# Dealing the last head group's maxima over 18 steps in place of 16, with the projection chain moved to match

## The chip, the cores and the metric

One core of a Trainium2 chip runs the kernel. The time is the device time of one execution in microseconds (us), from the first to the last instruction with what lies around them. The engines work side by side, each through its own list of instructions in order: TensorE (PE; its weight loads are PEld), VectorE (DVE), ScalarE (ACT), GpSimd (POOL) and SyncE (SP), which only issues transfers here. They wait for each other through semaphores, and an instruction that waits holds up all that stand behind it on its engine.

## The reference, cut to what matters

```
h = layernorm(x) * (1 + ca) + sa                      # x: 2048 tokens, 128 features
q, k, v = split(h @ W_attn + b_attn)                  # 16 heads of 8 features
att = softmax(q @ k.T / sqrt(8) + alibi_and_causal_mask)
x = x + ga * ((att @ v) @ W_proj + b_proj)
h = layernorm(x) * (1 + cb) + sb
probs = softmax(h @ router_w.T)                       # 8 experts, the best 2 are taken
y = silu(h @ w1[e]) @ w2[e] * expert_scale[e]         # 512 hidden features
x = x + gb * sum over the two experts of weight * y
```

The softmax is exact: each row's maximum is found and taken off before the exponential. The weights `ga`, `gb`, `sa` and so on come from a small conditioning product.

## The kernel before, in words

The heads are worked in four groups of four (`g` = 0 to 3). Tokens are cut into four chunks of 512 (`j`, or `c` in the later part), chunks into blocks of 128. The maxima of a row must be known before its exponentials, so attention has two passes over the scores.

**Pass 1, maxima.** A group has 72 tasks (`TASKS`, `NTASK`). A task multiplies a block row of queries by a chunk of keys on TensorE (line 724, masks at 697), into one of two slots of PSUM, and VectorE reduces it to row maxima (line 1040). When the last task of a chunk is done, VectorE makes the negated maxima (`nmax`, line 1048), GpSimd cuts them into three bf16 pieces (`cut_maxima`, lines 1445 to 1451), TensorE turns them (`turn`, line 746), ScalarE copies them to `rows` (line 1299), and SyncE sends them with four transfers into the stack of query rows `aug` (line 418). The scores of pass 2 then come with the maxima already taken off. The first step of a chunk waits for these rows (`rows_in`).

**Pass 2, steps.** A group has 36 steps (`STEPS`): chunk 0 starts at step 0, chunk 1 at 3, chunk 2 at 10, chunk 3 at 21 (`START`). A step has two halves `b`. In each half TensorE makes scores for keys by queries (line 795) into a ring of three PSUM slots, ScalarE takes exponentials (line 1326, four in a step), and TensorE multiplies the exponentials of the step before by the values (line 761). ScalarE copies a finished chunk out (`copy_values`, line 1293).

**The plan.** `plan` (line 98) says how many tasks of pass 1 are to be issued by the end of each half-step; it deals them by the share of pass 2 that has passed. Pass 1 runs `LEAD` = 41 tasks ahead, so that a group's pass 2 carries the first pass of the next. The last group (`g` = 3) has only its own 31 tasks left, numbers 41 to 71, and is done with them when the plan reaches 72, at the end of step 15. `turns` tells after which step a chunk's maxima are turned: the first step by which its tasks and four more are planned.

**What fills the second half of the last group.** From there on tables of step numbers place the next phase, for the first three chunks, into the steps on TensorE: `PROJECT` (line 648, two matmuls in each half), `TURN` (the normalized tokens, line 602), `LOGITS` (line 665) and `COUNT` (lines 674 and 677, which count tokens per expert; count 0 is for chunk 0, count 1 for chunks 1 and 2). `project` uses the PSUM banks of pass 1, so the first projection must come after the last task. VectorE has no steps there: it follows a fixed list. For each chunk it adds the projection (`residual`, line 1065), takes statistics, scales tokens after GpSimd's `deviation` (lines 1376 and 1385; then line 945), keeps the logits (1072) and ranks experts (`route`, 1082 to 1107). `place_part(0)` waits for count 0 and `place_part(1)` for count 1; they give each token its place in the tiles of its expert (1129 to 1144). Their order on VectorE is

```
residual(2)
place_part(0)
scale_tokens(2)
for k in range(1, 5):
    route(1, k)
...
place_part(1)
for j in range(DEEP - 1):
    stage(j)
```

`stage` copies an expert's first weights for a tile (line 1169), three tiles ahead at first, a fourth (`stage(3)`) only after `route(c, 5)` and the last chunk's `scale_sums`. GpSimd sends the tokens to their places with indirect transfers (`send_part`, lines 1480 and 1487): part 0 after `place_part(0)`, part 1 after `place_part(1)`; the deviation of the last chunk stands in the middle of part 1, behind twelve sends.

**The loop over 53 tiles** follows: TensorE turns a tile (870), multiplies by the first weights (`up`, 879), ScalarE takes silu (1353), TensorE multiplies by the second weights (`down`, 896), VectorE keeps the result (1177). The last chunk's projection, turn, logits and count stand among the tiles. At the end GpSimd gathers the results and VectorE joins them.

`ROUTE_EXP` places small exponentials of the routing on ScalarE at (step, exponential).

Of the kernel before, what the change touches and what calls it, by code (L numbers as in the profile page):

```python
# [44 lines left out]
NSTEP = len(STEPS)  # L45
# [7 lines left out]
NTASK = len(TASKS)  # L53
# [40 lines left out]
PASSED = [sum(PASS2[:p]) for p in range(NSTEP + 1)]  # L94
LEAD = max(TSTART[j + 1] + SETTLE + AHEAD - NTASK * PASSED[START[j]] // PASSED[NSTEP] for j in range(NC_))


def plan(first):

    if first:
        knots = [(PASSED[START[j]], TSTART[j + 1] + SETTLE0 + AHEAD0) for j in range(NC_)] + [(PASSED[NSTEP], NTASK + LEAD)]
        knots[1:1] = [(PASSED[1], TSTART[2] + SETTLE0)]
    else:
        knots = [(0, LEAD), (PASSED[NSTEP], NTASK + LEAD)]
    rows_ = []
    for p in range(NSTEP):
        row = []  # L110
        for b in range(PAIRS):
            x = PASSED[p] + PASS2[p] * (b + 1) // PAIRS
            for (x0, y0), (x1, y1) in zip(knots, knots[1:]):
                if x0 <= x <= x1:
                    want = y0 + (y1 - y0) * (x - x0) // (x1 - x0)
            row.append(want)
        rows_.append(row)
    return rows_


PLAN = {first: plan(first) for first in (True, False)}


def turns(p, first, last):

    found = []
    for u in range(2 * NC_ if not last else NC_):
        settled = TSTART[u % NC_ + 1] + NTASK * (u // NC_) + (SETTLE0 if first and u < NC_ else SETTLE)  # L130
        if first and u == 0:
            at = -1
        elif settled <= (0 if first else LEAD):
            continue
        else:
            steps = [q for q in range(NSTEP) if PLAN[first][q][-1] >= settled]
            if not steps:
                continue
            at = steps[0]
        if at == p:  # L140
            found.append(u)
    return found
# [12 lines left out]
LAST_OUT, LAST_IN, LAST_INVERT, LAST_BACK, LAST_INVERSE = [5, 11], [6, 12], [INVERT, 14], [9, 15], [10, 16]  # L155
LAST_SCALE = {13: 0, 18: 1}
DEVIATION_AT = {19: 0, 20: 1}
PROJECT = {16: 0, 18: 1, 23: 2}
TURN = {18: 0, 20: 1, 26: 2}
LOGITS = {19: 0, 21: 1, 27: 2}  # L160
ROUTE_EXP = {(20, 4): (0, 0), (23, 2): (1, 0), (25, 2): (0, 1), (28, 2): (2, 0), (30, 2): (1, 1), (34, 4): (2, 1)}
COUNT = {24: 0, 30: 1}


PARTS = [(0, TPC), (TPC, 3 * TPC), (3 * TPC, NT)]
# [50 lines left out]
def build(nc, a):  # L216
# [3 lines left out]
    with ExitStack() as ctx:  # L220
# [369 lines left out]
        def _(pe):  # L590
# [4 lines left out]
            for n, m in enumerate((0, 1, 3, 4)):  # L595
                last = mm(b1[:, 3, n:n + 1], wmod[:, m * C:(m + 1) * C], sil[:, :], start=True, stop=True)
# [87 lines left out]
            def group(g, first, last):  # L684
# [131 lines left out]
                def step(p):  # L816
                    if p == 0:
                        for u in turns(-1, first, last):
                            pass1(TSTART[u + 1] + SETTLE0)
                            turn(u)  # L820
                            pass1(TSTART[u + 1] + SETTLE0 + AHEAD0)
                    if p < NSTEP:
                        j, kbs = STEPS[p]
                        for b in range(PAIRS):
                            if p == START[j] and b == 0:
                                take(pe, rows_in[j % 2], HG * 16)
                            scores_and_maxima(p, b, min(PLAN[first][p][b], NTASK) if last else PLAN[first][p][b])
                            if p not in START:
                                value_products(p, b)
                            elif (p or g) and b == 0:  # L830
                                for half in range(PAIRS):
                                    value_products(p, half)
                                if p == 0 and not last:
                                    pe.sem_inc(aug_free, 1)
                            if last and p in PROJECT:
                                if p == min(PROJECT) and b == 0:
                                    assert at[0] == NTASK
                                    pe.wait_ge(s1_free, n_task[0] + SLOTS)
                                for half in range(2):
                                    project(PROJECT[p], 2 * b + half)  # L840
                        for u in turns(p, first, last):
                            turn(u)
                    if last:
                        if p in TURN:
                            turn_late(TURN[p])
                        if p in LOGITS:
                            logits(LOGITS[p])
                        if p in COUNT:
                            count(COUNT[p])
                    if last and p == NSTEP:  # L850
                        for b in range(PAIRS):
                            value_products(p, b)
# [70 lines left out]
        def _(dve):  # L923
# [94 lines left out]
            def group(g, first, last):  # L1018
                n_task, at = 0, 0 if first else LEAD
                for p in range(-1, NSTEP + 1):  # L1020
                    upto = PLAN[first][p][-1] if 0 <= p < NSTEP else 0
                    if last:
                        upto = min(upto, NTASK)
                    if g and p == INVERT:
# [6 lines left out]
                    while at < upto:  # L1031
                        k = at % NTASK
                        j, c, rs, b = TASKS[k]
# [574 lines left out]
```

## Time and profile before

| what | us |
|---|---|
| median of three runs | 560.79 (560.79 to 562.58) |
| the profiled execution, its time | 560.09 |
| its span, first to last instruction | 558.2 |
| busy in the span: PE, DVE, ACT, POOL | 490.7, 446.2, 396.6, 169.9 |
| last group of heads, from its first exponential | 340.58 |
| last maxima reduced on VectorE | 379.12 |
| attention ends (last copy of values begins) | 431.95 |
| last tile's products end, then gathers and joins | about 540 |

Read it by place: a busy share is a mean over phases that differ. What counts is which engine the others wait for in a stretch, and what stands behind the waiting instruction.

### The profile page before, as it was taken

To read this page: it belongs to the slowest core of one execution; us is meant where nothing else is said; L and a number is where in the kernel's file an instruction comes from. 1 tells how busy PE (TensorE), PEld (TensorE's weight loads), DVE (VectorE), ACT (ScalarE), POOL (GpSimd) and SP (SyncE) were. 2 spreads that over 40 slices of the span, in tenths; PEclk is the share of its full clock that TensorE was granted. 3 is DMA by queue.
4 is the path that set the end of the run, shared out by engine and by line. 5 is a ranking of instruction groups with operands and counts; after the bars stand their busy time and mean duration, and the time that the engine had idled before them with its cause. 6 is when DMAs were issued, how large, how long until landed. Compare 5 with 4: busy or idle time off the path is not lost.

```text
span 558.2 us, 16358 instructions
## 1 busy us (share of the span) xinstructions
PE 490.7 (88%) x6452; PEld 287.1 (51%) x6452; DVE 446.2 (80%) x775; ACT 396.6 (71%) x775; POOL 169.9 (30%) x293
## 2 busy tenths in 40 slices
PE   3756778889999999999999999999999998999960
PEld 2422233244344454444454445445434998999960
DVE  3689999989999999999999998995687646554442
ACT  3932366668989899898898897888789555555530
POOL 3410000000104112320044101066068852860864
PEclk9975799999999999999999999999899999999995
DMA  6593112000001460041320000010232222442432
GB/s 162 186 323 81 31 36 53 1 3 3 7 12 46 95 261 4 2 153 34 82 40 4 2 3 2 16 25 7 73 100 68 79 84 59 114 123 71 113 102 60
DMA packets 38267, 37.93 MB, mean 68 GB/s; under 512 B 7088, under 2 KB 33904, under 8 KB 37560
## 3 DMA queue, kind: packets, MB, share of 16 engines
q1 hardware_dynamic: 35808, 32.26, 20.3%
q0 software_dynamic: 2048, 4.20, 2.7%
q8 instruction: 53, 0.87, 0.7%
q10 hardware_dynamic: 336, 0.42, 0.2%
q14 instruction: 22, 0.18, 0.1%
HBM read 20.05 MB, written 16.61 MB: 66 GB/s over the span
## 4 chain that ended last, share of the span: by engine, by line
PE 55%; DVE 14%; ACT 5%; issue 2%; POOL 1%; DMA 1%; ACTq 0%; POOLq 0%; DVEq 0%
PE pv L761 18%; PE b L795 11%; DVE part L1040 9%; PE b L879 8%; PE b L896 8%; PE b L724 6%; ACT probs L1326 3%; PE b L697 3%; POOL raw L1508 1%; PE b L870 1%; ACT raw L1293 1%; DMA raw<-y_scratch,spots 0%; PE b L648 0%; PE b L746 0%; PE b L602 0%
## 5 line engine op out<-in xcount | busy, mean ns | idle before, releaser
L1326 ACT ACTIVATE probs<-b 128x512 f32<-128x512 f32 (+1 forms) x576 | 294.7, 571 | 65.1 <-PE b L795 29.9
L1040 DVE TENSOR_REDUCE part<-b 128x2 f32<-128x1024 f32 (+2 forms) x320 | 322.1, 1060 | 18.0 <-PE b L697 9.1
L761 PE MATMUL pv<-probs,v_cur 128*32 128x256 f32 (+1 forms) x2432 | 175.4, 370 | 0.0
L795 PE MATMUL b<-aug 55*128 55x256 bf16 (+1 forms) x1216 | 153.7, 264 | 9.3 <-ACT probs L1326 8.7
L724 PE MATMUL b<-aug 52*128 52x512 bf16 (+3 forms) x640 | 142.1, 364 | 20.5 <-DVE part L1040 18.3
L795 PEld LDWEIGHTS b<-aug 55*128 55x128 bf16 x1216 | 56.9, 94 | 119.6 <-ACT probs L1326 105.0
L761 PEld LDWEIGHTS pv<-probs,v_cur 128*32 128x32 f32 x2432 | 50.0, 108 | 49.7 <-ACT probs L1326 24.2
L724 PEld LDWEIGHTS b<-aug 52*128 52x128 bf16 x640 | 42.9, 94 | 39.8 <-DVE part L1040 29.8
L879 PE MATMUL b<-hTt,inverse 128*128 128x128 f32 x424 | 56.3, 276 | 0.8 <-ACT hTt L1347 0.8
L896 PE MATMUL b<-w2T_sb,hst 128*128 x424 | 56.2, 276 | 0.8 <-ACT hst L1353 0.8
L896 PEld LDWEIGHTS b<-w2T_sb,hst 128*128 128x128 f32 x424 | 51.6, 192 | 1.2 <-issue 1.2
L879 PEld LDWEIGHTS b<-hTt,inverse 128*128 128x128 f32 x424 | 51.5, 192 | 1.1 <-issue 1.0
L1353 ACT ACTIVATE hst<-b 128x512 f32<-128x512 f32 x53 | 31.6, 597 | 21.9 <-PE b L879 21.9
L1169 DVE COPY inverse<-aug 128x512 f32 x53 | 25.1, 474 | 24.4 <-issue 19.0
L1445 POOL CAST nmp<-nmax 128x16 bf16<-128x16 f32 x16 | 3.4, 211 | 124.6 <-POOLq L192 124.6
L1347 ACT ACTIVATE hTt<-b,modc 128x128 f32<-128x128 f32 x53 | 24.1, 456 | 22.7 <-PE b L870 22.7
L697 PE MATMUL b<-maskQ,identh 64*128 64x64 bf16 (+1 forms) x512 | 40.1, 210 | 0.0
L1177 DVE TENSOR_TENSOR aug<-b,gate 128x128 f32<-128x128 f32 x53 | 15.4, 290 | 25.4 <-PE b L896 22.8
L1487 POOL DMA_INDIRECT slot_scratch<-slots,spots x32 | 32.6, 1017 | 9.0 <-POOL pause L1480 9.0
L1480 POOL MEMSET pause<- 128x512 f32 (+1 forms) x56 | 25.4, 453 | 31.6 <-DMA y_scratch<-aug 29.6
L1508 POOL DMA_INDIRECT raw<-y_scratch,spots x32 | 31.2, 975 | 11.7 <-POOL pause L1480 6.8
L697 PEld LDWEIGHTS b<-maskQ,identh 64*128 64x128 bf16 x512 | 30.4, 99 | 6.6 <-issue 1.8
(151 smaller groups left out, 368.6 us busy)
## 6 DMA issues: line engine op xcount, KB each, us to landing
xt<-slot_scratch SPq DMA_DIRECT2D x53, 64.0 KB, 2.0
y_scratch<-aug SPq DMA_DIRECT2D x53, 64.0 KB, 1.6
slot_scratch<-slots SPq DMA_DIRECT2D x3, 1024.0 KB, 8.4
aug<-q_scratch SPq DMA_DIRECT2D x6, 384.0 KB
aug<-k_scratch SPq DMA_DIRECT2D x6, 384.0 KB
w2T_sb<-in_w2T SPq DMA_DIRECT2D x1, 2048.0 KB, 8.1
aug<-in_w1T SPq DMA_DIRECT2D x8, 256.0 KB
q_scratch<-pieces SPq DMA_DIRECT2D x4, 384.0 KB, 2.8
```

The lines of the kernel that those rows point to most:

```text
L697: return mm(bank[:, at_ + c0:at_ + c1], identh[k, h, :], table[k, h, c0:c1], start=False, stop=True, skip_group_check=True)
L724: ins = mm(bank[:, at_:at_ + w], q_aug[buf][n, b, t:t + P], k_aug[buf][n, b, c * CW:c * CW + w], start=True, stop=True)
L761: return mm(pv[32 * hh:32 * hh + 32, c0:c1], v_cur[:, kb, hh, :], probs[:, step_ % 2, hh, at_:at_ + c1 - c0], start=(kb == 0 and c0 == 0), ...
L795: ins = mm(bank[:, at_:at_ + w], k_aug[g % 2][n, pair, kb * P:kb * P + P], q_aug[g % 2][n, pair, j * CW + c0:j * CW + c1], start=True, sto ...
L879: last = mm(b1[:, j % 2, f * P:(f + 1) * P], w1s[:, k, f * P:(f + 1) * P], hTt[:, j % 2, :], start=True, stop=True)
L896: last = mm(b1[:, 2 + j % 2, 0:C], hst[:, j % 2, f, :], w2T[:, ds(e * FC + f, 1), :], start=(f == 0), stop=(f == FC - 1))
L1040: ins = nc.vector.tensor_reduce(dst, b1[:, slot:slot + 2, at_:at_ + w], AX.X, ALU.max)
L1326: nc.scalar.activation(out, b2[:, (n2 - 1) % RING2, 0:PAIRS * w].rearrange("p (b t) -> p b t", b=PAIRS), ACT.Exp).then_inc(exp_done, 1)
L1353: nc.scalar.activation(hst[:, j % 2, :, :].rearrange("p f t -> p (f t)"), b1[:, j % 2, :], ACT.Silu).then_inc(silu_s, 1)
L1480: own.inc(nc.gpsimd.memset(pause[:, 0:columns], 0.0))
L1487: nc.gpsimd.indirect_dma_start(slot_dram, bass.IndirectOffsetOnAxis(ap=spots[:, b, n:n + 1], axis=0), slots[:, n, :], None).then_inc(sent_ ...
L1508: nc.gpsimd.indirect_dma_start(yfin[:, n, b, :], None, y_dram[0:BASE[k + 1] * P, :], bass.IndirectOffsetOnAxis(ap=spots[:, b, n:n + 1], ax ...
```

## The change

The last group gets its own plan. A third knot makes it reach all 72 tasks at the end of step 17 (18 steps) in place of step 15. The first three chunks' projections move from steps 16, 18, 23 to 18, 20, 24, the tokens' turns from 18, 20, 26 to 20, 22, 27, logits from 19, 21, 27 to 21, 23, 28, counts from 24, 30 to 26, 32, and the routing exponentials with them. The other groups' plans are what they were.

```diff
-def plan(first):
+LAST_TASKS = 18
+
+
+def plan(first, last):
...
+    elif last:
+        knots = [(0, LEAD), (PASSED[LAST_TASKS], NTASK), (PASSED[NSTEP], NTASK + LEAD)]
     else:
         knots = [(0, LEAD), (PASSED[NSTEP], NTASK + LEAD)]
...
-PLAN = {first: plan(first) for first in (True, False)}
+PLAN = {kind: plan(*kind) for kind in ((True, False), (False, False), (False, True))}
...
-PROJECT = {16: 0, 18: 1, 23: 2}
-TURN = {18: 0, 20: 1, 26: 2}
...
-COUNT = {24: 0, 30: 1}
+PROJECT = {18: 0, 20: 1, 24: 2}
+TURN = {20: 0, 22: 1, 27: 2}
...
+COUNT = {26: 0, 32: 1}
```

By the new plan the half-steps of the last group issue these tasks: before, steps 0 to 15 hold 31 tasks, with two in the second half of step 8 and none in the first halves of steps 2 and 9; now steps 0 to 17 hold them, one or none in each half, none in the first halves of steps 0, 6, 9 and 12 and in the second half of step 2. The turn of chunk 2's maxima moves from step 2 to step 3, that of chunk 3's from step 17 to step 19, and step 21 still reads them first. All lines from 98 on move down by three to five.

**On VectorE**, the last group of heads. `part<-b` are the reductions of the tasks, `sums` the reciprocals of two softmax sums at steps 8 and 14, `nmax` the last chunk's maxima and `x_sb<-b` the first chunk's residual. Before:

```order
L1040 TENSOR_REDUCE part<-b 128x2 x14
L1026 RECIPROCAL sums<-sums 128x64
L1030 RECIPROCAL sums<-sums 128x16
L1040 TENSOR_REDUCE part<-b 128x2 x14
L1030 RECIPROCAL sums<-sums 128x16
L1040 TENSOR_REDUCE part<-b 128x2 x4
L1046 MEMSET tick 128x1
L1048 TENSOR_REDUCE nmax<-part 128x16
L1065 TENSOR_TENSOR x_sb<-b,x_sb 128x512
```

And with the change:

```order
L1045 TENSOR_REDUCE part<-b 128x2 x12
L1031 RECIPROCAL sums<-sums 128x64
L1035 RECIPROCAL sums<-sums 128x16
L1045 TENSOR_REDUCE part<-b 128x2 x10
L1035 RECIPROCAL sums<-sums 128x16
L1045 TENSOR_REDUCE part<-b 128x2 x10
L1051 MEMSET tick 128x1
L1053 TENSOR_REDUCE nmax<-part 128x16
L1070 TENSOR_TENSOR x_sb<-b,x_sb 128x512
```

After the second `sums` reciprocal of step 14 there now stand ten reductions in place of four.

**On TensorE**, the turn of chunk 3's maxima (`identb,nmp`) and what follows it. `b<-aug` are scores, `maskT_sb` their masks, `pv` value products, `wproj_sb,yn` a projection's two matmuls. Before, it is followed by step 18:

```order
L746 MATMUL b<-identb,nmp 12x128 x4
L795 MATMUL b<-aug 128x256 x2
L697 MATMUL b<-maskT_sb,identh 128x64 x2
L697 MATMUL b<-maskT_sb,identh 128x128 x2
L795 MATMUL b<-aug 128x256 x2
L697 MATMUL b<-maskT_sb,identh 128x64 x2
L697 MATMUL b<-maskT_sb,identh 128x128 x2
L761 MATMUL pv<-probs,v_cur 32x256 x4
L648 MATMUL b<-wproj_sb,yn 128x128 x2
L795 MATMUL b<-aug 128x256 x4
L761 MATMUL pv<-probs,v_cur 32x256 x4
L648 MATMUL b<-wproj_sb,yn 128x128 x2
```

With the change it is followed by step 20, whose second projection half is the last row here; the first turn of tokens and the scores of step 21 come right behind:

```order
L751 MATMUL b<-identb,nmp 12x128 x4
L800 MATMUL b<-aug 128x128 x2
L702 MATMUL b<-maskT_sb,identh 128x64 x2
L702 MATMUL b<-maskT_sb,identh 128x128 x2
L800 MATMUL b<-aug 128x128 x2
L702 MATMUL b<-maskT_sb,identh 128x64 x2
L702 MATMUL b<-maskT_sb,identh 128x128 x2
L766 MATMUL pv<-probs,v_cur 32x256 x4
L653 MATMUL b<-wproj_sb,yn 128x128 x2
L800 MATMUL b<-aug 128x128 x4
L766 MATMUL pv<-probs,v_cur 32x128 x8
L653 MATMUL b<-wproj_sb,yn 128x128 x2
```

The turn of the maxima stood three steps ahead of step 21; now one step lies between.

**On TensorE**, from the end of count 0 (`both,full`) to the third turn of tokens (`ident_sb,slots`). Each pair of scores and value products is a half-step. Before:

```order
L677 MATMUL b<-both,full 128x8
L795 MATMUL b<-aug 128x256 x4
L761 MATMUL pv<-probs,v_cur 32x256 x4
L795 MATMUL b<-aug 128x256 x4
L761 MATMUL pv<-probs,v_cur 32x256 x4
L795 MATMUL b<-aug 128x256 x4
L761 MATMUL pv<-probs,v_cur 32x256 x4
L795 MATMUL b<-aug 128x256 x4
L761 MATMUL pv<-probs,v_cur 32x256 x4
L602 MATMUL b<-ident_sb,slots 128x128 x4
```

With the change:

```order
L682 MATMUL b<-both,full 128x8
L800 MATMUL b<-aug 128x256 x4
L766 MATMUL pv<-probs,v_cur 32x256 x4
L800 MATMUL b<-aug 128x256 x4
L766 MATMUL pv<-probs,v_cur 32x256 x4
L607 MATMUL b<-ident_sb,slots 128x128 x4
```

Two steps lay between them, now one does. Behind the third turn, count 1 stood at the end of the fourth step (27 to 30), and stands at the end of the fifth (28 to 32).

## Rows read from the trace of the kernel before

**Rows 1.** Busy time by stretch (us): count in brackets, then granted clock and DMA share.

```profile
340.58:378.85 38.27, 36.53 (x574) 17.48 (x574) 36.19 (x39) 33.98 (x68) 12.39 (x16) 1.00 0.10 17
388.10:391.00 2.90, 2.77 (x45) 1.66 (x42) 1.36 (x9) 2.57 (x5) 1.27 (x2) 1.00 0.00 0
396.87:400.28 3.41, 3.41 (x29) 0.87 (x32) 3.17 (x10) 2.38 (x6) 0.00 (x0) 0.50 0.22 77
```

**Rows 2.** Timeline of TensorE: value products that close half-steps; start, length, count.

```profile
369.52 0.64 PE L761 MATMUL pv<-probs,v_cur 128*32 128x256 f32 x8
...
370.63 0.64 PE L761 MATMUL pv<-probs,v_cur 128*32 128x256 f32 x8
...
416.65 0.64 PE L761 MATMUL pv<-probs,v_cur 128*32 128x256 f32 x8
...
418.66 0.64 PE L761 MATMUL pv<-probs,v_cur 128*32 128x256 f32 x8
```

**Rows 3.** Timeline of TensorE: scores before and after the half-step with two tasks.

```profile
360.29 0.31 PE L795 MATMUL b<-aug 55*128 55x128 bf16 x4
...
362.37 0.23 PE L795 MATMUL b<-aug 55*128 55x128 bf16 x2
```

**Rows 4.** Timeline of TensorE, steps 17 to 21.

```profile
383.35 0.39 PE L746 MATMUL b<-identb,nmp 128*12 128x128 bf16 x4
383.67 0.66 PE L795 MATMUL b<-aug 55*128 55x256 bf16 x2
...
387.72 0.28 PE L795 MATMUL b<-aug 55*128 55x256 bf16 x2
...
390.22 1.06 PE L665 MATMUL b<-rwT_sb,hT 128*128 128x8 f32 x8
391.21 0.23 PE L795 MATMUL b<-aug 55*128 55x128 bf16 x2
...
393.58 0.39 PE L795 MATMUL b<-aug 55*128 55x256 bf16 x4
```

**Rows 5.** Timeline of SyncE: the transfers of the last chunk's maxima.

```profile
384.54 2.77 SPq L418 DMA_DIRECT2D aug<-rows  x4
```

**Rows 6.** Timeline of TensorE, steps 22 and 23.

```profile
396.43 0.54 PE L795 MATMUL b<-aug 55*128 55x256 bf16 x4
...
400.68 0.71 PE L648 MATMUL b<-wproj_sb,yn 128*128 128x128 f32 x4
401.32 0.39 PE L795 MATMUL b<-aug 55*128 55x256 bf16 x4
```

**Rows 7.** Timeline of TensorE: third turn, step 33, and a tile's first layer.

```profile
410.17 0.66 PE L602 MATMUL b<-ident_sb,slots 128*128 128x128 f32 x4 [0.87 <-DVE slots L945]
410.76 0.39 PE L795 MATMUL b<-aug 55*128 55x256 bf16 x4
...
424.66 0.37 PE L795 MATMUL b<-aug 55*128 55x256 bf16 x2
...
438.73 1.06 PE L879 MATMUL b<-hTt,inverse 128*128 128x128 f32 x8
```

**Rows 8.** Timeline of VectorE: placing, scaling, and copies of expert weights.

```profile
406.05 0.19 DVE L1129 TENSOR_TENSOR more<-b,steps 128x64 f32<-128x64 f32 x1
...
408.92 1.20 DVE L945 TENSOR_SCALAR slots<-x_sb,mv,rstd 128x128 f32<-128x128 f32 x4
...
420.71 0.23 DVE L1129 TENSOR_TENSOR more<-b,steps 128x64 f32<-128x64 f32 x1 [0.15 <-PE b L677]
...
425.15 0.44 DVE L1169 COPY inverse<-aug 128x512 f32 x1 [0.97 <-DVE spots L1144]
...
436.23 0.43 DVE L1169 COPY inverse<-aug 128x512 f32 x1
```

**Rows 9.** Timeline of GpSimd: first send of part 1, last chunk's deviation.

```profile
424.33 0.52 POOL L1480 MEMSET pause<- 128x512 f32 x1 [0.44 <-DVE spots L1144]
...
446.95 0.23 POOL L1376 TENSOR_SCALAR rstd<-mv 128x4 f32<-128x4 f32 x1 [1.05 <-DVE mv L936]
```

More of the change, by code:

```diff
@@ L135, in turns @@
         else:
-            steps = [q for q in range(NSTEP) if PLAN[first][q][-1] >= settled]
+            steps = [q for q in range(NSTEP) if PLAN[first, last][q][-1] >= settled]
             if not steps:
@@ L157 @@
 DEVIATION_AT = {19: 0, 20: 1}
-PROJECT = {16: 0, 18: 1, 23: 2}
-TURN = {18: 0, 20: 1, 26: 2}
-LOGITS = {19: 0, 21: 1, 27: 2}
-ROUTE_EXP = {(20, 4): (0, 0), (23, 2): (1, 0), (25, 2): (0, 1), (28, 2): (2, 0), (30, 2): (1, 1), (34, 4): (2, 1)}
-COUNT = {24: 0, 30: 1}
+PROJECT = {18: 0, 20: 1, 24: 2}
+TURN = {20: 0, 22: 1, 27: 2}
+LOGITS = {21: 0, 23: 1, 28: 2}
+ROUTE_EXP = {(22, 4): (0, 0), (25, 2): (1, 0), (27, 2): (0, 1), (29, 2): (2, 0), (31, 2): (1, 1), (34, 4): (2, 1)}
+COUNT = {26: 0, 32: 1}
 PARTS = [(0, TPC), (TPC, 3 * TPC), (3 * TPC, NT)]
@@ L826, in step @@
                                 take(pe, rows_in[j % 2], HG * 16)
-                            scores_and_maxima(p, b, min(PLAN[first][p][b], NTASK) if last else PLAN[first][p][b])
+                            scores_and_maxima(p, b, min(PLAN[first, last][p][b], NTASK) if last else PLAN[first, last][p][b])
                             if p not in START:
@@ L1020, in group @@
                 for p in range(-1, NSTEP + 1):
-                    upto = PLAN[first][p][-1] if 0 <= p < NSTEP else 0
+                    upto = PLAN[first, last][p][-1] if 0 <= p < NSTEP else 0
                     if last:
```

## The prediction, as it was put on record

> **What bounds the kernel now.** I read the kernel from its last phase backwards, because only the last group of heads changes. First, the busy times by stretch. While the last group's maxima run (the first 16 steps, 32 half-steps) TensorE is busy 36.53 of 38.27 us, VectorE 36.19 and ScalarE 33.98 [rows 1]: three engines in lockstep, none of which can be relieved alone. Second, the timeline of TensorE: one half-step with a maxima task takes 1.11 us (from 369.52 to 370.63), one without takes about 1.01 (416.65 to 418.66 is two of them) [rows 2]; for a whole plain step I use 2.04, since ScalarE's copies come between. So a task costs the step only 0.1 us when it is alone in its half-step. Where two tasks share one, in step 8, the half-step takes 2.08 us (360.29 to 362.37) [rows 3]. Third, the waits on VectorE and GpSimd after the maxima. In the second half of the group VectorE does the routing of the first three chunks, and each piece of it waits for a matmul that stands at a fixed step. There the two engines chase each other: TensorE waits 0.87 us for VectorE's normalized tokens at 410.17 [rows 7], VectorE waits 0.15 us for the second count at 420.71 [rows 8], and GpSimd 0.44 us for the places at 424.33 and 1.05 us at 446.95 [rows 9]. That second half is what this change must be judged by.
>
> **The change, part by part.** All sums are in the profiled execution, which took 560.09 us (span 558.2 and 1.9 around it). The median of the runs is 560.79, so I work out a shift and add it to the median.
>
> *Dealing the tasks.* The 31 tasks stood in 32 half-steps, one with two tasks and two empty. They will stand in 36, none doubled and five empty. The program of steps 0 to 17 thus gains two ordinary task halves (2.22 us), loses the doubled one (2.08) and gains three empty ones (3.03): +3.2 us for two more steps. The exponentials of step 16 begin at 378.85, those of step 18 will begin at 382.05, and their scores about 0.5 us earlier: 381.5. Before, step 18's scores began at 383.67 [rows 4]. That is a lead of 2.2 us, but before, the lead-in held one projection and one turn of the maxima, which are still to come.
>
> *Steps 18 to 23.* Prices: a projection half 0.64 us (400.68 to 401.32) [rows 6]; turning the maxima 0.32 (383.35 to 383.67) and logits 0.99 (390.22 to 391.21) [rows 4]; turning tokens 0.59 (410.17 to 410.76) [rows 7]. Step 18 took 4.05 and loses its turn: 3.46, to 385.0. Step 19 took 3.49, loses logits and gains the maxima's turn: 2.82, to 387.8. Step 20 took 2.37 and gains a projection, 1.28: 3.65, so TensorE is ready for step 21 at 391.4.
>
> *A new wait there.* Step 21 is the first to read the last chunk's maxima. They used to be turned after step 17 and will be turned after step 19, one step before use. Before, the turn began at 383.35 [rows 4], ScalarE's copy followed, SyncE issued four transfers from 384.54 over 2.77 us [rows 5], and from 388.10 on nothing moves on the DMA engines [rows 1]: 4.75 us from turn to landing. In the new order the turn begins at 387.5, the rows land at 392.2, and TensorE, with the whole of step 21 queued behind this wait, stands for 0.8 us. The last of the four issues starts about 386.7. The Trainium skill, page "DMA: Bandwidth & Descriptors", section "Anatomy of one DMA", gives about 2.0 us fixed for a transfer on GpSimd's path; by it the landing would be 0.6 us later and this wait 1.4. I keep the trace's 4.75.
>
> Step 21 took 2.85 with some waiting for ScalarE; without the tokens' turn just ahead of it I take 2.5, to 394.7. Step 22 is 2.04 with tokens (2.63), step 23 is 2.04 with logits (3.03): step 24 starts near 400.4. Step 24 with the third projection is 3.1 (part of the projection hides in ScalarE's pace), step 25 is 2.04, step 26 with the first count 2.24: 407.8.
>
> *The third chunk.* Its tokens are turned one step later (27), but its count stands two steps later (26). VectorE cannot place part 0 before this count. Placing takes 2.87 us (406.05 to 408.92) and scaling the third chunk 1.20 [rows 8], so the tokens are there at 411.9, while TensorE has finished step 27 at 409.8. The 0.87 us wait becomes 2.1 us; ScalarE's exponentials are queued behind it. Step 28 begins at 412.5 after the transposes. From there to the second count lie steps 28 to 32, one step fewer than the six from 410.76 to 424.66 [rows 7]: 13.90 - 2.04 = 11.86, so step 33 begins at 424.4. TensorE's attention ends within 0.3 us of where it did. The whole lead is gone, eaten by the two waits.
>
> *The second count is what costs.* It used to stand after step 30 and VectorE got it at 420.71 [rows 8]. It will stand after step 32: 424.45. VectorE will be ready for it near 422.3 (10.4 us after the scaled tokens, as before from 408.92 + 1.20 to 420.71 - 0.15) and idles. So all that follows it slips by 3.7 us, in two queues. (a) VectorE: the copies of weights begin at 425.15; the fourth one begins at 436.23 and ends at 436.66 [rows 8], and TensorE wants it at 438.73 [rows 7]. 436.66 + 3.7 = 440.4 against 438.5: a wait of 1.9 us in the loop over expert tiles. (b) GpSimd: the sends of part 1 start at 424.33 and the last chunk's deviation is behind twelve of them, where GpSimd had 1.05 us to spare [rows 9]. It comes 3.7 - 1.05 = 2.7 us late, and TensorE's turn of the last chunk waits for it already now. The two overlap: 2.7 us in all, and the loop after it is dense matmul that gives nothing back.
>
> *The clock.* From 396.87 to 400.28 the granted clock was 0.5, 1.2 GHz, with TensorE busy all the while [rows 1]; three half-steps took 4.25 us (396.43 to 400.68) [rows 6] where about 2.95 is usual, so it costs 1.3 us. It came behind a stretch of narrow logits matmuls and a short wait. My sums above hold no such stretch, so they count its end as gained. The new waits of 0.8, 2.1 and 1.9 us leave the engine far less to do than that one did, so I expect at least one such stretch again, at the same price. The Trainium skill, page "TensorE: Matmul & The Clock Gate", section "Part 1: The HAM clock gate", says the same in words: full speed is granted for activity. Total: 2.7 + 1.3 = +4.0 us, 564.8.
>
> **Rivals.**
> - *Late counts, but full clock throughout.* The waits stay, no slow stretch: +2.7, 563.5. For it: the wait of 0.87 us at the third turn passed without a drop. Against: 2.1 us is more than twice that. 22%.
> - *The slip is covered, no change.* If VectorE's chain and step 33 come 1 to 2 us sooner than I think (a shorter wait at step 28), GpSimd's 1.05 us and VectorE's 2.1 us of spare time before the fourth copy cover most of it: 560.8 to 562.5. 19%.
> - *Faster.* The first sixteen steps are where VectorE and TensorE are fullest; if the lead of 2.2 us survives to the end of attention and the slow clock does not come back, the time is 560.8 - 2.2 - 1.3 = 557.3. This decides only if the second count ends by 421.8, which is 2.6 us sooner than worked out. 8%.
> - *Worse.* Slow stretches behind two of the waits, one of them in the loop over tiles, which is bound by TensorE: 566 to 568. 6%.
>
> **Numbers.** My forecast, late counts with one slow stretch, has 45%, alone 562.8 to 566.8. The 80% range takes in the covered case and most of the double one: 560.8 to 567.5. What this kernel can show against no change is about 0.5%, 2.8 us: slower is the forecast, half of the full-clock rival and the worse case, 0.62; same 0.29; faster 0.09.
>
> **What the changed profile would show.** Step 18's scores near 381.5; a wait of TensorE at the scores of step 21 on the transfer of rows; a wait near 2 us for VectorE's scaled tokens ahead of the third turn; VectorE waiting for the second count, which lands near 424.5; TensorE waiting for a weight copy early in the loop over tiles; GpSimd no longer waiting at the last deviation; and somewhere a 0.5 of granted clock. I am wrong if steps 3 to 8, where VectorE was the later engine, give back more than the 0.9 us counted, or if the slow stretch does not return.

## Result and profile after

| | us | of before |
|---|---|---|
| before, six runs | 561.37 (560.79 to 564.69) | |
| after, six runs | 570.70 (566.80 to 572.04) | 1.0127 (1.0092 to 1.0163) |
| forecast | 564.8 (560.8 to 567.5) | |

The change makes the kernel slower. The medians stand 9.3 us apart, a quotient of 1.0166; the ratio in the table, 1.0127, is an estimate of its own over the executions of both kernels, with its 95% interval in brackets, and not that quotient. By either, the side was right, the size was not, and the time lies outside the range. The profiled execution took 571.49 us, its span is 569.6: 11.4 us above the profiled one of before.

I begin with where the 11.4 us lie. The first exponential of the last group began at 340.58 before and begins at 343.01 now. Nothing ahead of it was changed, so 2.4 us belong to something else (see the clock, below). In what follows, "from S0" is a time less this start. From S0 to the end of the span before took 217.6 us and after takes 226.6: +9.0 us is what there is to explain.

First the busy times by stretch of the changed kernel (busy and count for PE, PEld, DVE, ACT and POOL, then the granted clock, 1.00 for 2.4 GHz and 0.50 for 1.2, then the DMA share and GB/s). The first stretch runs from S0 to step 18's scores, the fourth is the end of the idle time before the third turn of tokens, and the others begin or end near a change of the clock.

```profile
343.01:384.47 41.46, 39.77 (x614) 18.32 (x607) 35.80 (x39) 37.88 (x76) 15.23 (x18) 1.00 0.09 16
397.80:401.20 3.40, 3.40 (x26) 0.95 (x26) 3.23 (x10) 2.62 (x5) 0.00 (x0) 0.50 0.27 77
401.20:414.10 12.90, 12.53 (x141) 5.60 (x143) 8.61 (x37) 10.34 (x23) 1.27 (x2) 1.00 0.28 87
416.08:416.75 0.67, 0.00 (x0) 0.00 (x1) 0.67 (x4) 0.00 (x0) 0.36 (x2) 1.00 0.84 202
418.27:428.51 10.24, 10.09 (x74) 3.63 (x72) 7.62 (x28) 6.47 (x13) 8.56 (x12) 0.50 0.12 40
428.51:433.52 5.01, 5.01 (x73) 2.09 (x73) 0.83 (x5) 4.17 (x9) 1.69 (x3) 1.00 0.16 48
```

Step 18's scores begin 41.46 us from S0, 0.5 us later than forecast. A stretch at clock 0.50 like that of [rows 1] stands at 397.80, with the same length. A second one begins at 418.27 and lasts 10.24 us, three times as long, with TensorE busy for 10.09 of them.

The timeline of TensorE in the changed kernel shows the waits (in brackets the idle time and what ended it) and the long stretch. These rows answer to [rows 4] and [rows 7].

```profile
395.23 0.40 PE L800 MATMUL b<-aug 55*128 55x256 bf16 x4 [0.95 <-PEq L197]
...
416.75 0.66 PE L607 MATMUL b<-ident_sb,slots 128*128 128x128 f32 x4 [2.17 <-DVE slots L950]
...
419.30 1.08 PE L766 MATMUL pv<-probs,v_cur 128*32 128x256 f32 x8
420.31 1.88 PE L670 MATMUL b<-rwT_sb,hT 128*128 128x8 f32 x8
...
424.21 1.08 PE L766 MATMUL pv<-probs,v_cur 128*32 128x256 f32 x8
425.23 0.61 PE L800 MATMUL b<-aug 55*128 55x256 bf16 x4
425.77 1.08 PE L766 MATMUL pv<-probs,v_cur 128*32 128x256 f32 x8
...
448.79 1.16 PE L884 MATMUL b<-hTt,inverse 128*128 128x128 f32 x8 [1.59 <-DVE inverse L1174]
```

All three forecast waits of TensorE are there at nearly their forecast size: 0.95 us ahead of step 21 (0.8), 2.17 at the third turn (2.1), 1.59 for a copy of weights (1.9). In the slow stretch the value products start every 1.56 us, where a half-step took about 1.01 in [rows 2], and the logits take 1.88 us against 1.06 in [rows 4].

The timeline of SyncE of the changed kernel, for [rows 5], and below it that of VectorE, for [rows 8]:

```profile
391.24 2.77 SPq L423 DMA_DIRECT2D aug<-rows  x4
```

```profile
412.59 0.23 DVE L1134 TENSOR_TENSOR more<-b,steps 128x64 f32<-128x64 f32 x1 [0.54 <-PE b L682]
...
415.50 1.20 DVE L950 TENSOR_SCALAR slots<-x_sb,mv,rstd 128x128 f32<-128x128 f32 x4
...
432.96 0.23 DVE L1134 TENSOR_TENSOR more<-b,steps 128x64 f32<-128x64 f32 x1 [4.04 <-PE b L682]
...
448.31 0.43 DVE L1174 COPY inverse<-aug 128x512 f32 x1
```

Placing and scaling take 2.91 and 1.20 us (forecast 2.87 and 1.20). The second count comes at 432.96, 89.95 us from S0. Before it was 80.13, and I had forecast 83.87. VectorE idles 4.04 us for it.

GpSimd in the changed kernel, from the first send of part 1 to the last chunk's deviation, for [rows 9]:

```profile
436.42 0.52 POOL L1485 MEMSET pause<- 128x512 f32 x1 [5.94 <-DVE spots L1149]
437.22 0.97 POOL L1492 DMA_INDIRECT slot_scratch<-slots,spots  x1 [0.28 <-POOL pause L1485]
...
457.42 1.05 POOL L1492 DMA_INDIRECT slot_scratch<-slots,spots  x1 [0.28 <-POOL pause L1485]
458.50 0.26 POOL L1381 TENSOR_SCALAR rstd<-mv 128x4 f32<-128x4 f32 x1
```

The deviation no longer waits for VectorE: it comes right behind the twelfth send. So GpSimd is now what the end hangs on, and the chain that ended last, on the page of the changed kernel, says the same (shares of the span):

```profile
PE 20%; POOL 5%; DVE 2%; issue 2%; DMA 1%; ACT 0%; POOLq 0%; DVEq 0%; ACTq 0%
PE b L901 7%; PE b L884 7%; PE pv L766 2%; POOL slot_scratch L1492 2%; PE b L800 2%; POOL pause L1485 1%; POOL raw L1513 1%; PE b L875 1%; PE b L670 1%; DMA raw<-y_scratch,spots 0%; DVE slots L950 0%; PE b L607 0%; DMA y_scratch<-aug 0%; PE b L653 0%; POOLq L225 0%
```

The sends and their pauses (L1492, L1485) stand among its first lines. From the count onward everything is late together: the count by 9.8 us, less the 1.05 us that GpSimd had to spare [rows 9], is 8.8, and the end is late by 9.0. The 1.05 us are not a fixed reserve, though. In e1 below, with the count 7.9 us late and the end 8.1, GpSimd still waits 1.05 us there for VectorE's mean, and in e10, with 3.1 and 2.9, 0.31 us: VectorE is late by as much as the count, and the spare time covers little or nothing.

### The profile page after: what moved, and what is told of

It is laid out like the page before. It is cut to its first block and busy times, and to the rows that moved or that the text cites. A ratio compares the mean times of both kernels' runs of the same rounds, so it can differ in the third digit from the quotient of the medians.

```text
span 569.6 us, 16358 instructions
## 1 busy us (share of the span) xinstructions
PE 497.6 (87%) x6452; PEld 289.0 (51%) x6452; DVE 446.5 (78%) x775; ACT 397.3 (70%) x775; POOL 170.0 (30%) x293
## 5 line engine op out<-in xcount | busy, mean ns | idle before, releaser
L766 PE MATMUL pv<-probs,v_cur 128*32 128x256 f32 (+1 forms) x2432 | 178.8, 376 | 0.0
L800 PE MATMUL b<-aug 55*128 55x256 bf16 (+1 forms) x1216 | 155.5, 268 | 10.5 <-ACT probs L1331 9.0
L729 PE MATMUL b<-aug 52*128 52x512 bf16 (+3 forms) x640 | 143.6, 366 | 19.6 <-DVE part L1045 17.4
L1485 POOL MEMSET pause<- 128x512 f32 (+1 forms) x56 | 25.5, 455 | 37.9 <-DMA y_scratch<-aug 29.6
L1492 POOL DMA_INDIRECT slot_scratch<-slots,spots x32 | 32.9, 1028 | 8.9 <-POOL pause L1485 8.9
```

Of the source, the lines that this page charges most:

```text
L729: ins = mm(bank[:, at_:at_ + w], q_aug[buf][n, b, t:t + P], k_aug[buf][n, b, c * CW:c * CW + w], start=True, stop=True)
L766: return mm(pv[32 * hh:32 * hh + 32, c0:c1], v_cur[:, kb, hh, :], probs[:, step_ % 2, hh, at_:at_ + c1 - c0], start=(kb == 0 and c0 == 0), ...
L800: ins = mm(bank[:, at_:at_ + w], k_aug[g % 2][n, pair, kb * P:kb * P + P], q_aug[g % 2][n, pair, j * CW + c0:j * CW + c1], start=True, sto ...
L1485: own.inc(nc.gpsimd.memset(pause[:, 0:columns], 0.0))
L1492: nc.gpsimd.indirect_dma_start(slot_dram, bass.IndirectOffsetOnAxis(ap=spots[:, b, n:n + 1], axis=0), slots[:, n, :], None).then_inc(sent_ ...
```

## Experiments

Times are medians, with the ratio to the kernel before in the same session on the same chip and its 95% interval; as above, it is not the quotient of the medians. That kernel's medians there were 562.86 (e1 to e4), 562.85 (e5 to e8), 562.88 (e9 to e11) and 563.41 (e12, e13). The traces are compared by times from S0, since S0 itself moves (340.6 to 343.6 us) with slow stretches in the first groups. "Step 33" is that step's first exponential and "count 1" the second count's arrival on VectorE, both from S0; "tail" is the span's end less S0. The last column is in us from the start of the span. It leaves out the half clock in which every trace ends, from 202 to 212 us after S0 on, when the last tiles are done.

| | median | ratio (95%) | step 33 | count 1 | tail | half clock from S0 on, but for the last: start, length |
|---|---|---|---|---|---|---|
| before | 561.37 | | 84.8 | 80.1 | 217.6 | 396.9, 3.4 |
| after | 570.70 | 1.0127 (1.0092, 1.0163) | 90.5 | 90.0 | 226.6 | 397.8, 3.4; 418.3, 10.2 |
| e1_tables | 569.31 | 1.0103 (1.0043, 1.0164) | 88.6 | 88.1 | 225.7 | 414.5, 10.2; 448.7, 3.4 |
| e2_fill | 565.82 | 1.0041 (1.0010, 1.0071) | 85.6 | 85.1 | 221.4 | none |
| e3_counts | 567.21 | 1.0076 (1.0051, 1.0101) | 88.3 | 85.7 | 222.9 | 414.4, 10.2 |
| e4_rows | 568.72 | 1.0108 (1.0083, 1.0134) | 88.3 | 87.8 | 224.3 | 415.3, 10.2 |
| e5_turn28 | 565.19 | 1.0048 (1.0027, 1.0069) | 83.6 | 83.1 | 221.0 | 440.9, 3.4 |
| e6_old_places | 562.99 | 1.0005 (0.9980, 1.0030) | 85.6 | 80.9 | 218.4 | 400.5, 3.4 |
| e7_turn28_counts | 563.10 | 1.0009 (0.9987, 1.0031) | 83.5 | 81.3 | 218.3 | none |
| e8_before_fill | 561.69 | 1.0005 (0.9973, 1.0038) | 84.8 | 80.2 | 217.7 | 399.4, 3.4 |
| e9_candidate | 565.80 | 1.0033 (1.0011, 1.0056) | 87.1 | 84.5 | 221.7 | 396.9, 10.2 |
| e10_before_turn25 | 565.34 | 1.0029 (1.0006, 1.0052) | 87.7 | 83.3 | 220.5 | 400.1, 3.4; 413.7, 3.4 |
| e11_half_fill | 567.62 | 1.0074 (1.0048, 1.0100) | 85.6 | 85.1 | 221.6 | none |
| e12_turn25_logits26 | 564.88 | 1.0041 (1.0012, 1.0070) | 87.7 | 83.2 | 220.7 | 397.1, 3.4; 410.7, 3.4 |
| e13_logits29 | 568.02 | 1.0097 (1.0059, 1.0135) | 86.5 | 86.1 | 222.5 | 414.8, 3.4 |

### Which part of the change costs: e1 and e6

e1 keeps the old dealing and takes the new tables.

```diff
-PROJECT = {16: 0, 18: 1, 23: 2}
+PROJECT = {18: 0, 20: 1, 24: 2}
...
-COUNT = {24: 0, 30: 1}
+COUNT = {26: 0, 32: 1}
```

> The old plan (maxima dealt over 16 steps) with the new tables of projections, turns, logits, exponentials and counts. It separates the deal from the places. If the late places are the cost (count 1 two steps later, third turn waiting for VectorE): about 570, as the changed kernel, since count 1 comes after step 32 all the same. If the deal itself costs the time, by making three engines' steps slower or by turning chunk 3's maxima late: 561 to 562, as before.

e6 is the reverse: it keeps the new dealing, but the third chunk's turn, its logits and both counts stand at their old steps, the first two chunks one step off (the first projection two), and the last chunk's maxima are turned after step 18.

```diff
-            at = steps[0]
+            at = 18 if last and u == 3 else steps[0]
...
+PROJECT = {18: 0, 19: 1, 23: 2}
+TURN = {19: 0, 21: 1, 26: 2}
+LOGITS = {20: 0, 22: 1, 27: 2}
...
+COUNT = {24: 0, 30: 1}
```

> The deal over 18 steps, with everything behind it as near to the old places as it allows: maxima turned after 18; projections 18, 19, 23; turns 19, 21, 26; logits 20, 22, 27; counts 24, 30. If the deal itself is harmless and the late places with their clock are the cost: 561 to 563, no worse than before; VectorE gets count 1 within 1 us of its old time. If the deal itself costs: 566 or more.

The tables alone have a ratio of 1.0103. The dealing with the old places has 1.0005, which can't be told from no change, and a tail 0.8 us longer. So dealing the maxima over 18 steps is about free. What costs is where the next phase's work was moved to.

### The counts and the rows: e3 and e4

e3 moves only the counts of the changed kernel one step earlier, e4 only the turn of the last chunk's maxima.

```diff
-COUNT = {26: 0, 32: 1}
+COUNT = {25: 0, 31: 1}
```

> The changed kernel with the two counts one step earlier (25 and 31). If VectorE's wait for count 1 (4.04 us) is handed on to the end through GpSimd's sends and the weight copies: one step less, 2 to 3 us faster, 568, and the third turn's wait falls by 0.5. If the counts are beside the point and the clock decides: the same slow stretch and the same time within 0.5 us.

```diff
-            at = steps[0]
+            at = 18 if last and u == 3 else steps[0]
```

> The changed kernel with chunk 3's maxima turned after step 18 in place of 19, so that their four transfers have a step more. If the wait of 0.95 us ahead of step 21 is on the path: it goes, and the time falls by 0.9 us, to 569.8. If that idle time is also what brings the half clock at 397.8: 2.2 us, to 568.5. If it is hidden by the later waits for VectorE: no change.

e3 brings the count to VectorE 4.2 us sooner than after (85.7 for 90.0 from S0; 1.3 of it because this trace has no stretch near 398) and the tail is 3.7 shorter: the end follows the count. The wait at the third turn falls from 2.17 to 1.59 us. In e4 the wait ahead of step 21 is gone, yet the third turn waits 2.15 us as in after, since VectorE's tokens depend on count 0. The tail is 2.3 us shorter; 1.3 of these are the price of the slow stretch at 397.8, which e4's trace happens not to have, and 0.9 is the wait. Both keep the stretch of 10.2 us.

### The wait at the third turn and the clock: e2, e11, e5, e8

e2 adds work to the changed kernel: eight matmuls of zeros and ones, whose result nobody reads, ahead of the third turn. They take 1.90 us, and the third turn's wait behind them is 0.33 us.

```diff
+FILL = 8
...
             def turn_late(c):
-                pe.wait_ge(xn_s, NC_ + c + 1)
                 if 0 < c < NC_ - 1:
                     pe.wait_ge(hT_s, NC_ + c)
+                if c == 2:
+                    for _ in range(FILL):
+                        mm(banks(c)[1], identb[:, :], full[:, None, :].to_broadcast([P, TPC, P]), start=True, stop=True, skip_group_check=True)
+                pe.wait_ge(xn_s, NC_ + c + 1)
```

> The changed kernel with eight filler matmuls (128x512, bf16, into the bank that the turn overwrites) just ahead of the third turn's wait for VectorE, where TensorE stood idle for 2.17 us. They take about the time of that wait, so the wait itself is not shortened. If the stretch at half clock from 418.27 to 428.51 comes from that idle time and costs what its half-steps say (1.55 us for 1.02): the stretch is gone and the time falls by 3 to 4 us, to 567. If only the waits and the late counts matter: no change, 570.7.

The filler and the third turn in e2's timeline of TensorE:

```profile
412.67 1.90 PE L663 MATMUL b<-full,identb 128*128 128x512 bf16 x8
414.90 0.66 PE L608 MATMUL b<-ident_sb,slots 128*128 128x128 f32 x4 [0.33 <-DVE slots L954]
```

The windows of e2, from step 23 to the fill and from the third turn on:

```profile
396.00:412.50 16.50, 16.13 (x180) 7.46 (x177) 12.48 (x48) 14.30 (x31) 2.05 (x3) 1.00 0.29 89
414.90:427.00 12.10, 11.85 (x132) 4.80 (x132) 9.11 (x35) 10.45 (x22) 10.41 (x14) 1.00 0.13 43
```

Full clock everywhere. The tokens come no sooner by the filler, yet the tail is 5.2 us shorter than after's (221.4 for 226.6). That trace has neither of the two slow stretches. From S0 the third turn is at 72.4 for 73.7: 1.3 us for the stretch ahead of it. The filler stands behind that stretch and can't have removed it; up to there e2 and after are the same program, so this part is a difference between executions. Behind the turn the long one is missing: that gains 3.6 by step 33 and 3.9 by the end. What is left over before, 3.8 us, is the price of the late places at full clock, net of the one slow stretch that before's own trace has.

e11 is the same with `FILL = 4`. The wait is 1.19 us.

> The changed kernel with four fillers in place of eight ahead of the third turn, so that TensorE stands about 1.2 us there. If the full 2.17 us of idle time is needed for the half clock: no long stretch, 565 to 567, as with eight. If any extra idle time there brings it: 569 to 571.

Its profiled execution has no slow stretch and took 564.15 us, at a mean clock of 0.962. But only one more of its ten runs is like that (564.07); the others took 566.7 to 568.6 at 0.950 to 0.954. A mean clock lower by 0.008 is about 9 us more at half clock, and the time is about 3.6 us longer, which is what a stretch of 10.2 us cost above. That is an estimate from the run list, as the places of these slow stretches were not recorded; by it four fillers mostly did not keep the long stretch away. The median, 567.62, lies between the two times that were expected, 565 to 567 without a long stretch and 569 to 571 with one. So the clock is not a fixed property of the program: with the same instructions it falls in some executions and not in others.

e5 moves the third turn one step later, so that the tokens are there when TensorE comes to them (the diff leaves out a routing exponential that moves with them); e8 fills the 0.87 us of the kernel before with four of the same extra matmuls.

```diff
-TURN = {20: 0, 22: 1, 27: 2}
-LOGITS = {21: 0, 23: 1, 28: 2}
+TURN = {20: 0, 22: 1, 28: 2}
+LOGITS = {21: 0, 23: 1, 29: 2}
...
```

> The changed kernel with the third turn and the third logits one step later (28 and 29), so that TensorE works on step 28 while VectorE scales the tokens, in place of standing 2.17 us. No filler work. If idle TensorE before a run of narrow logits brings the half clock: no slow stretch of 10 us, and 564 to 566, as with the filler. If lateness of the chain is all that counts: the third chunk's logits come no sooner than before, nothing is gained, 570.

> The kernel before with four filler matmuls (128x512, bf16) ahead of the third turn, where it waits 0.87 us. It is the control for the filler. If a filler only helps where idle time brings the half clock: no change, 560.5 to 563, since no slow stretch follows that wait here. If filler matmuls help by something else, such as keeping the clock up later in general: 1 to 3 us faster.

e5 has no wait at the third turn and no stretch behind it, and gets back more than half: 1.0048. The count still stands at step 32 and comes 2.9 us later than before's; the tail is 3.4 us over before's, with a short slow stretch among the tiles. e8 is like before in everything (217.7). So the extra matmuls do nothing where no slow stretch follows the wait; what the late tokens themselves cost before, a filler can't show.

### Both together: e7, and a search for better: e9

e7 is e5 with the rows turned after step 18 and the counts at 25 and 31.

```diff
-COUNT = {26: 0, 32: 1}
+COUNT = {25: 0, 31: 1}
```

> The third turn at 28, logits at 29, chunk 3's maxima turned after 18, counts at 25 and 31: every wait that was named made shorter, the deal and the projections left as in the change. If the waits and the clock together are the whole loss: 562 to 564, with no slow stretch. If one of the pieces was not a cause: what it was to give is missing, 565 or more.

Its ratio is 1.0009, with the wait at the third turn gone, the counts earlier and no slow stretch in its trace. Attention ends 90.1 us from S0, 1.2 us sooner than before, and the end is not sooner, since the count comes at 81.3 for 80.1.

e9 was a try for a faster kernel, with the second projection and turn closer, the counts at 24 and 31 and the last chunk's maxima turned after step 18.

```diff
...
+PROJECT = {18: 0, 19: 1, 23: 2}
+TURN = {20: 0, 21: 1, 27: 2}
+LOGITS = {21: 0, 22: 1, 28: 2}
...
+COUNT = {24: 0, 31: 1}
```

> A try for a version that keeps the lead of the deal: maxima turned after 18, projections 18, 19, 23, turns 20, 21, 27, logits 21, 22, 28, counts 24 and 31. VectorE gets logits 1 about 2 us sooner than in the version with turn 28, so count 1 should find it in time. If the deal is worth its 1 to 2 us at the start of step 18: 560 to 562, as before or 0.2% faster. If VectorE's fixed chain after the first projection, which the deal delays by two steps, sets the end: 562.5 to 564, no better than the old places.

Its ratio is 1.0033 and its median of 565.8 is above both times that were expected: a miss. TensorE waited 1.05 us at its second turn, and 2.3 us later, at 396.9, the clock fell for 10.2 us. No version was faster than the kernel before.

```profile
394.60 0.65 PE L607 MATMUL b<-ident_sb,slots 128*128 128x128 f32 x4 [1.05 <-DVE slots L950]
```

### Why 10.2 us: e10, e12, e13

e10 makes a long wait in the kernel before by turning the third chunk at 25.

```diff
-TURN = {18: 0, 20: 1, 26: 2}
+TURN = {18: 0, 20: 1, 25: 2}
```

> The kernel before with its third turn one step too early (25 in place of 26) and nothing else changed: TensorE will stand about 3 us for VectorE's tokens in place of 0.87. If only the wait counts: 2.1 us later at count 1, of which 1.05 is covered on GpSimd: 562 to 563.5. If the idle time also brings the long stretch at half clock: a stretch of about 10 us from near 413 on, and 566 to 568.

```profile
413.19 0.66 PE L602 MATMUL b<-ident_sb,slots 128*128 128x128 f32 x4 [2.94 <-DVE slots L945]
```

The wait was 2.94 us, longer than after's, and the slow stretch behind it only 3.4 us. A long stretch had been expected: a miss. The length of the wait does not set the length of the stretch. Laying the traces side by side gave another candidate. Four lines from four timelines of TensorE, of e9, e3, e1 and e10 in this order, each of a group of logits:

```profile
398.66 1.88 PE L670 MATMUL b<-rwT_sb,hT 128*128 128x8 f32 x8
```

```profile
416.89 1.88 PE L670 MATMUL b<-rwT_sb,hT 128*128 128x8 f32 x8
```

```profile
419.08 1.88 PE L665 MATMUL b<-rwT_sb,hT 128*128 128x8 f32 x8
```

```profile
419.01 1.06 PE L665 MATMUL b<-rwT_sb,hT 128*128 128x8 f32 x8
```

e9's clock fell at 396.9 and e3's at 414.4: a group of logits (eight matmuls of 8 columns) begins 1.7 and 2.4 us later; in after and e4 it is 2.0. e10's fell at 413.7, was back at 417.1, and the logits begin at 419.0, 5.3 us later. The six stretches of 3.4 us in this phase (before, after, e6, e8, two in e10) hold no logits, and but for the one behind e10's wait each begins within about 0.6 us behind a group of them. So four of the five long stretches have logits in their first 3.4 us and none of the short ones has. The fifth, e1's, does not fit: its logits begin 4.5 us into it. Two kernels were to test this: e12 is e10 with the logits at 26 in place of 27, e13 the changed kernel with the third chunk's logits at 29 in place of 28 (and the routing exponential behind them).

```diff
-LOGITS = {19: 0, 21: 1, 27: 2}
+LOGITS = {19: 0, 21: 1, 26: 2}
```

> The kernel before with the third turn of tokens at step 25 as in the run before it, and its logits at 26 in place of 27, one step behind the turn. Theory A, the narrow logits matmuls keep the granted clock down: TensorE waits 2.9 us for the tokens again, the clock falls to 0.5 right behind, and because the logits (eight matmuls of 8 columns) now begin inside the first 3.4 us of it, they take 1.88 us in place of 1.06 and the stretch lasts 10.2 us, not 3.4. Four us more than the run with logits at 27: about 569. Theory B, the length of a stretch is chance or hangs on the length of the wait: 3.4 us again and about 565.

```diff
-LOGITS = {21: 0, 23: 1, 28: 2}
+LOGITS = {21: 0, 23: 1, 29: 2}
...
```

> The changed kernel with the third chunk's logits at step 29 in place of 28, two steps behind its turn; the turn keeps its wait of 2.2 us. VectorE has 4.0 us to spare before the second count, so the later logits delay nothing of their own. Theory A, logits inside the first part of a slow stretch prolong it: the clock falls at the turn but is back after 3.4 us, logits take 1.06 us, and some 2.5 us of the changed kernel's loss come back: near 568 where the changed kernel had 570.7. Theory B, chance or the length of the wait: a stretch of 10.2 us again, near 570.

Windows of e13 in the slow stretch and behind it, and its timeline of TensorE:

```profile
414.84:418.24 3.40, 3.40 (x28) 0.76 (x24) 3.09 (x11) 2.67 (x6) 2.83 (x5) 0.50 0.11 39
418.24:424.24 6.00, 6.00 (x72) 2.62 (x68) 2.66 (x11) 5.05 (x12) 5.16 (x8) 1.00 0.11 36
```

```profile
413.77 0.66 PE L607 MATMUL b<-ident_sb,slots 128*128 128x128 f32 x4 [2.16 <-DVE slots L950]
...
419.57 1.06 PE L670 MATMUL b<-rwT_sb,hT 128*128 128x8 f32 x8
```

With the same wait of 2.16 us the stretch lasts 3.4 us, as the candidate says, and step 33 comes 4.0 us sooner than after's: 1.3 of it is the earlier stretch, which is missing from this trace too, and 2.7 the shorter one. The median, 568.02, is between after and before. But the profiled execution is the fastest of seven: one more is like it (566.2), and two took 571.1 at a mean clock of 0.941, as long as after. e12 did not make the case it was meant for: the clock fell 0.17 us sooner than in e10 against the program (in the turn itself, 410.71), was back at 414.12, and the logits begin at 414.19, just behind. 3.4 us and 564.88 are what either theory gives for that; but three of its twelve runs took 567.3 to 568.8 at a mean clock of 0.941 for the profiled one's 0.957, near the 569 that was expected with a long stretch. Of e10's ten runs none is below 0.948. That fits the candidate, but no trace says where those stretches lay. So the candidate rests on one trace in which it was foretold, e13, and on eleven stretches of nine traces in which it was read afterwards, with e1 against it. It is supported, not proven; chance between executions remains the rival, and e11 shows that there is chance.

## Why the prediction missed

**What was right.** The mechanism of the waits holds step by step. The dealing gave step 18 a lead of 1.6 us (its scores 41.46 us from S0 for 43.09), forecast 2.2. The transfers of rows were issued at once, and step 21 stands 0.95 us for them (0.8). The third turn waits 2.17 us (2.1), VectorE idles for the second count, a weight copy is late by 1.59 us (1.9; with the 438.73 of [rows 7] in place of the 438.5 in the sum, 1.7), and GpSimd's deviation stops waiting. e6 and e1 show that the places, not the dealing, cost; e3 and e7 that the end follows the count. The rivals "covered" and "faster" are out, and so is full clock throughout. "TensorE's attention ends within 0.3 us of where it did" did not hold: it ends 5.7 us later from S0, and 0.9 us later even in e2, without a slow stretch.

**The term that failed: the clock.** "I expect at least one such stretch again, at the same price", 1.3 us. There were two. The one of 397.8 did cost 1.3, as worked out (e2 against after at the third turn). The one at the third turn's wait cost 3.9. Together 5.2 where 1.3 stood. Two faults lie in this step. The heavier is that I took the old stretch's 3.4 us for the length of any other: behind the third turn after, e1, e3 and e4 have 10.2 us, and e9 has it behind its second turn. The lighter is that I took the old stretch as gone, on no row. In after's trace one of the same length stands near its old place. Here luck has a part: after, e2, e3, e5, e11 and e13 are the same program up to there, and in the other five traces it is missing, while before, e8, e10 and e12, also one program up to their stretch near 56.3 us from S0, all have it. The rival "worse" had two stretches, but up to its 568 it gave them at most 4.5 us together, one of them in the loop over tiles, and 6% for it was too little.

**The late places at full clock: 2.7 forecast, 3.8 measured** (e2 against before). The sum had the third turn at 71.3 us from S0 and e2 has it at 72.4. Of this, 0.6 is there at step 21 and comes from the transfer of rows; the other 0.5 is there when the first count reaches VectorE. I had 4.75 us from turn to landing; in after, scores begin at 395.23, 5.24 us behind the turn at 389.99, and SyncE's first issue came 1.25 behind it (1.19 before). The Trainium skill, page "DMA: Bandwidth & Descriptors", section "Anatomy of one DMA", gives its 2.0 us for GpSimd's path, and these transfers are issued by SyncE; the 0.6 us more that the prediction worked out from it, 5.35 in all, an estimate, is nearer to the 5.24 measured than the 4.75 up to the trace's last busy DMA engine. From the third turn to step 33 the sum was right within 0.1, so count 1 was 1.2 late with it (85.1 for 83.9).

**The ledger of the profiled executions.** 3.8 for late places and 5.2 for the clock are 9.0, by construction, since both are differences over e2; 2.4 more is the later start of the last group. That makes 11.4, the difference of the spans. The 2.4 is not from the change: after's trace has a half-clock stretch of 6.8 us at 73.5, in the first groups, which the trace of before has not, and e4, e7 and e8 have one of 3.4 or 6.8 us there as well, e8 being the kernel before with a filler more than 330 us later. It is in the scatter of both kernels, and so the traces stand 11.4 apart and the medians 9.3. How the 9.3 split between places and clock is known only as far as the one trace of each kernel stands for its other runs.

**What would have told.** A range that took the clock's price from both sides. Its trace showed one stretch of 3.4 us with TensorE busy all through it [rows 1] and no bound on how long another may last; the one of 27.3 us from 35.1 on, in the first group, did not enter the range. By the rows of after, where half-steps take 1.56 for 1.01, a stretch costs about 35% of its length: 1.2 us for 3.4, 3.6 for 10.2, near the 1.3 and 3.9 that the experiments gave. A long stretch in place of the short one, and the old one returned, would have put the sum at 2.7 + 3.9 + 1.3, 568.7. Another part is the base: I added to 560.79, a median of three runs, and the same kernel's median over 35 runs was 562.85.

**Open.** Why the stretch behind the third turn lasts 10.2 us and not 3.4. What makes the clock fall in some executions of a program and not in others (e11), and whether the narrow logits themselves prolong a slow stretch or something that moves with them. Also whether in the unprofiled runs the slow stretches lie where the profiled ones have them: for those only the mean clock is known (after: 0.945 or lower in five of six, 0.954 in the fastest, 566.8).

## What to carry to other kernels

When a phase is filled from a table of steps, the item to hold in place is the one that another engine's list waits for, here the counts. Dealing the filler work differently was about free; two steps on the counts, with the clock, were not. A wait on TensorE is to be priced twice, once as time, and once for the clock that may fall behind it, with a length bounded from both sides by the longest and shortest slow stretch of the whole trace. If a wait can't be removed, keeping the narrow matmuls a step away from it may help: in e13's trace the stretch was short, but two of its seven runs were as slow as after.

## What was not expected of the hardware

- At half clock TensorE was busy 10.09 of 10.24 us and stayed slow. In e13, the same program but for the step of one group of logits and of the exponential behind it, it was back at full clock after 3.4 us. The Trainium skill, page "TensorE: Matmul & The Clock Gate", section "Part 1: The HAM clock gate", ties the full clock to TensorE's activity. If activity is read as the busy share, this stretch goes against it, and the measurement decides.
- The stretch at 397.8 began right behind the second chunk's logits (396.67 and 1.06 us long in after), as in before, e6, e8, e10 and e12. Only in after had a wait of 0.95 us come shortly ahead of it; in e6 the longest was 0.59, in the other four 0.36 to 0.37. In e1, e2, e3, e4, e5, e7, e11 and e13 it was missing with nearly the same work ahead of it. That a clock falls behind matmuls of 8 columns with hardly a wait was not expected, nor that with one program, up to there that of after, e2, e3, e5, e11 and e13, it falls in one trace of six.
- Waits and clock are not tied one to one. A wait of 2.94 us was followed by 3.4 us of half clock (e10), one of 1.05 us by 10.2 (e9), one of 1.19 us by none in the profiled execution (e11), one of 2.44 us for a copy of weights by none (e13, at 443.78), and two of 0.9 us by none (e5 ahead of step 21, before at the third turn).
- Executions of the kernel before, the same program on the same chip, scatter from 560.4 to 566.3 us, and their mean clocks go with it: 0.959 to 0.960 for the five fastest of 18, 0.95 for the nine slowest.
